# Loading a stage's constants one stage earlier, and issuing a load ahead of a store in one DMA queue

## What is computed

```python
x = x + conv3(conv2(conv1(group_norm(x))))      # 3x3, weights mixed per sample from 4 experts
# second layer, v = group_norm(x):
X  = dht2d(v)                                   # Hartley transform: real part minus imaginary part of the FFT
Xc = X[:, :, 96:160, 96:160]                    # 64 x 64 modes; Xrc the same of the flipped transform
x_even, x_odd = (Xc + Xrc) * 0.5, (Xc - Xrc) * 0.5
total = einsum('bixy,ioxy->boxy', x_even, kernel) + einsum('bixy,ioxy->boxy', x_odd, flipped_kernel)
out = dht2d(pad(total), is_inverse=True) + bias # back to 256 x 256
x = x + out
```

## Time and profile before

| | |
|---|---|
| median of 3 runs | 4815.48 us (4814.95 to 4819.85) |
| the profiled execution | 4815.04 us, span 4813.2 us |
| TensorE busy over the span | 4398.2 us (91%) |
| VectorE, ScalarE, GpSimd | 77%, 53%, 36% |
| DMA, inverse stage (4111.6 to 4813.2 us) | 396 GB/s |
| DMA, mixing stage (3783.0 to 4111.6 us) | 168 GB/s |

### The profile page before, as it was taken

The page is one execution under the profiler, slowest core; times in us unless marked ns, Lnnn a source line. Parts: engine busy times, 40 slices in busy tenths (PEclk is TensorE's granted clock), DMA queues, the critical chain, the costliest instruction groups (busy, mean ns, idle before and its releaser), DMA issues. The chain is left out here.

```text
span 4813.2 us, 126429 instructions
## 1 busy us (share of the span) xinstructions
PE 4398.2 (91%) x43186; PEld 2826.4 (59%) x43186; DVE 3683.3 (77%) x5717; ACT 2549.5 (53%) x4890; POOL 1726.5 (36%) x1963
## 2 busy tenths in 40 slices
PE   5999999999999999999999999995887677799998
PEld 2555555555555555555555545454777677688887
DVE  5877877878778787787877877777888799565555
ACT  2666666566566665666666656565787300233333
POOL 4455454554545545455454554544000000000000
PEclk9999999999999999999999999998999788899999
DMA  5867668676686766867767777679999798899999
GB/s 143 198 153 176 168 158 191 147 181 168 151 191 155 183 166 144 191 158 181 170 149 181 171 166 170 146 182 261 330 338 328 186 198 159 326 406 404 406 406 378
DMA packets 730995, 1042.38 MB, mean 217 GB/s; under 512 B 149184, under 2 KB 612832, under 8 KB 680928
## 3 DMA queue, kind: packets, MB, share of 16 engines
q1 hardware_dynamic: 658064, 1011.11, 75.8%
q10 hardware_dynamic: 72784, 29.63, 2.4%
HBM read 746.67 MB, written 293.88 MB: 216 GB/s over the span
## 5 line engine op out<-in xcount | busy, mean ns | idle before, releaser
L350 PE MATMUL bank<-ring_B,w_now 128*64 128x512 f16 (+1 forms) x14283 | 3091.0, 377 | 90.9 <-DVE ring_B L292 60.2
L350 PE MATMUL bank<-ring_A,w_now 128*64 128x512 f16 (+1 forms) x14283 | 3091.2, 377 | 0.0
L350 PEld LDWEIGHTS bank<-ring_B,w_now 128*64 128x64 f16 x14283 | 1547.5, 109 | 1517.7 <-issue 73.0
L350 PEld LDWEIGHTS bank<-ring_A,w_now 128*64 128x64 f16 x14283 | 1547.4, 109 | 0.0
L288 ACT COPY ring_B<-ring_A 64x516 f32<-64x516 f32 x1059 | 657.7, 621 | 944.3 <-DVE ring_A L574 906.0
L574 DVE SCALAR_TENSOR_TENSOR ring_A<-bank,ring_A 128x512 f16<-128x512 f32 (+1 forms) x1027 | 700.5, 682 | 463.8 <-ACT ring_A L418 444.1
L418 ACT ACTIVATE ring_A<-bank 128x512 f16<-128x512 f32 (+1 forms) x1027 | 603.0, 587 | 275.3 <-PE bank L350 273.0
L728 POOL TENSOR_TENSOR ring_A<-xn,ring_A 128x512 f16<-128x512 f32 x515 | 584.7, 1135 | 94.6 <-POOL xn L726 92.7
L1427 DVE SCALAR_TENSOR_TENSOR i_ot<-i_ob,i_bias_bc,i_xt 128x512 f32<-128x512 f32 x512 | 363.8, 747 | 294.8 <-DMA i_xt<-x 184.5
L1371 PE MATMUL i_ob<-i_back,i_u 128*128 128x256 f32 x2048 | 529.2, 381 | 10.8 <-DVE i_ot L1427 9.3
L290 ACT COPY ring_B<-ring_A 64x516 f32<-64x516 f32 x705 | 438.3, 622 | 8.1
(11 more groups left out here) (161 smaller groups left out, 5148.8 us busy)
## 6 DMA issues: line engine op xcount, KB each, us to landing
f_xt<-x SPq DMA_DIRECT2D x128, 1024.0 KB, 6.0
i_xt<-x SPq DMA_DIRECT2D x128, 1024.0 KB, 16.2
out<-i_ot SPq DMA_DIRECT2D x128, 1024.0 KB, 14.2
st_in_A<-in_x SPq DMA_DIRECT2D x65, 1024.0 KB, 7.4
st_in_B<-in_x SPq DMA_DIRECT2D x65, 1024.0 KB, 7.8
x_in_A<-in_x SPq DMA_DIRECT2D x324, 192.0 KB, 4.0
res_A<-in_x SPq DMA_DIRECT2D x324, 192.0 KB, 5.2
res_B<-in_x SPq DMA_DIRECT2D x324, 192.0 KB, 5.0
```

Source lines behind the costliest of these rows:

```text
L350: last = nc.tensor.matmul(dst[64 * half:64 * half + 64, 0:nb * IMG], w_now[n][:, w, 64 * dx:64 * dx + 64], r[side][:, kind, s0:s0 + nb, dx ...
```

## The change

Two edits, both in the diff below. First, `back` and `bias_bc` are allocated ahead of the forward stage and kept to the end, and their two loads are issued by ScalarE, as the first instructions of its stream in `build_mix`, with a semaphore of their own; ScalarE waits for them at the end of its stream there. The two loads and the semaphore `here` disappear from `build_inverse`, with the waits of TensorE and VectorE on it. Second, in each group of `build_inverse` SP issues the load of `x1` first and the store behind it; both stand behind the same wait for `o_ready`.

```diff
@@ build_mix
         @block.scalar
         def _(act):
+            act.dma_start(back[:], spec[:, OFF_BACK:OFF_BACK + 2 * IMG]).then_inc(consts_here, 16)
+            act.dma_start(bias_bc[:], bias.rearrange("c a b -> (a b) c").to_broadcast([P, C])).then_inc(consts_here, 16)
+
             for k in range(NCK):
                 act.wait_ge(emptied, k + 3)
                 for g in range(2):
                     y0 = 32 * g + k * T
                     act.dma_start(t_d[:, y0:y0 + T].rearrange("b t o x -> (t o) b x"), to[:, g]).then_inc(gone, 16)
+            act.wait_ge(consts_here, 32)
@@ build_inverse
-        back = sb("back", [P, 2 * IMG])
-        bias_bc = sb("bias_bc", [P, C])
...
             load_t(0)
-            sp.dma_start(back[:], spec[:, OFF_BACK:OFF_BACK + 2 * IMG]).then_inc(here, 16)
-            sp.dma_start(bias_bc[:], bias.rearrange("c a b -> (a b) c").to_broadcast([P, C])).then_inc(here, 16)
             for g in range(NB):
                 sp.dma_start(xt[g][:], xv[0, :, 4 * g:4 * g + 4, :]).then_inc(x_here[g], 16)
...
                     sp.wait_ge(o_ready, n0 + (4 * g + 4 + O_READY))
+                    if not last or g < 8 - NB:
+                        at = s if g < 8 - NB else sp.snap(s + 1)
+                        k = 4 * ((g + NB) % 8)
+                        sp.dma_start(xt[g % NB][:], xv[at, :, k:k + 4, :]).then_inc(x_here[g % NB], 16)
                     sp.dma_start(ov[s, :, 4 * g:4 * g + 4, :], ot[g % NB][:]).then_inc(gone[g % NB], 16)
-                    if last and g >= 8 - NB:
-                        continue
-                    at = s if g < 8 - NB else sp.snap(s + 1)
-                    k = 4 * ((g + NB) % 8)
-                    sp.dma_start(xt[g % NB][:], xv[at, :, k:k + 4, :]).then_inc(x_here[g % NB], 16)
...
         @block.tensor
         def _(pe):
-            pe.wait_ge(here, 32)
-
...
@@ build_inverse, vector
-            dve.wait_ge(here, 32)
             with dve.Fori(0, S) as s:
@@ build
+        back = ctx.enter_context(nc.sbuf_tensor("i_back", [P, 2 * IMG], f32))
+        bias_bc = ctx.enter_context(nc.sbuf_tensor("i_bias_bc", [P, C], f32))
```

More of the change, by code:

```diff
@@ L1169, in _, with build_mix @@
             sample(S - 1, 1, True)
-def build_mix(nc, f_d, fm_d, w, t_d, wt, wr, S):
+def build_mix(nc, f_d, fm_d, w, t_d, wt, wr, back, bias_bc, spec, bias, S):
     f32 = mybir.dt.float32
@@ L1194, in build_mix @@
         gone = sem("gone")
+        consts_here = sem("consts_here")
         block = ctx.enter_context(nc.Block())
@@ L1277, in _, with build_inverse @@
                     act.dma_start(t_d[:, y0:y0 + T].rearrange("b t o x -> (t o) b x"), to[:, g]).then_inc(gone, 16)
-def build_inverse(nc, t_d, x1d, bias, spec, out_d, S):
+            act.wait_ge(consts_here, 32)
+def build_inverse(nc, t_d, x1d, back, bias_bc, out_d, S):
     f32 = mybir.dt.float32
@@ L1307, in build_inverse @@
         ob = [ps(f"ob{i}", [P, 512]) for i in range(4)]
-        here, zeroed, u_ps, u_ready, o_ps, o_ready = (sem(n) for n in ("here", "zeroed", "u_ps", "u_ready", "o_ps", "o_ready"))
+        zeroed, u_ps, u_ready, o_ps, o_ready = (sem(n) for n in ("zeroed", "u_ps", "u_ready", "o_ps", "o_ready"))
         t_here = sem("t_here")
@@ L1441, in build @@
     with ExitStack() as ctx:
[L1443 to L1447, removed]
+        back = ctx.enter_context(nc.sbuf_tensor("i_back", [P, 2 * IMG], f32))
+        bias_bc = ctx.enter_context(nc.sbuf_tensor("i_bias_bc", [P, C], f32))
+        with ExitStack() as inner:
+            weights = lambda name: inner.enter_context(nc.sbuf_tensor(name, [P, C, ROWS, M], f32))
+            wt, wr = [weights(f"m_wt{i}") for i in range(2)], weights("m_wr")
+            build_forward(nc, x1, x1_stats, spec, modes, middle, mode_w, wt[0], wr, S)
+            build_mix(nc, modes, middle, mode_w, mixed_modes, wt, wr, back, bias_bc, spec, bias, S)
+        build_inverse(nc, mixed_modes, x1, back, bias_bc, out, S)
 _INS = ["x", "L0_conv_w_c1", "L0_conv_w_c2", "L0_conv_weight1", "L0_conv_weight2", "L0_conv_weight3",
```

## The result

| | before | changed | ratio |
|---|---|---|---|
| median of 12 runs each | 4818.9 us (4808.6 to 4826.6) | 4801.1 us (4797.1 to 4812.3) | 0.9968, 95% interval 0.9959 to 0.9977 |
| the same, measured once more (14 and 8 runs) | 4812.9 us | 4795.7 us | 0.997, 0.9953 to 0.9987 |
| profiled execution, span | 4813.2 us | 4803.7 us | |

The change is faster by 0.32%, some 15 us (the two medians themselves lie 17.8 us apart, 17.2 us in the second measurement), and the forecast of 4813.3 us (4806.7 to 4820.2) is missed.

The account below looks back on a forecast made before the run. The prediction took TensorE, then from about 4286 us the DMA engines, to bound the inverse. 4815.04 - 2.2 + 0 + 0 = 4812.8 us, with the median 0.44 us above: 4813.3 us, range 4806.7 to 4820.2.

Parts of the forecast that it names:

- The bound: Inverse stage: TensorE sets the pace at first, DMA engines from about 4286 us, 42.94 us a sample at 404 GB/s.
- Edit 1 at the inverse's entry: Inverse's start: TensorE's first product no longer waits for the bias, 2.2 us earlier, all kept to the end.
- Edit 1 at the mixing's entry: Mixing's start: the two constant loads hide behind the clearing of ft, cost 0, at most 6.9 us.
- The Trainium skill's rule on shared engines: Mixing's entry: moving loads to another queue gains no bandwidth; forecast not to bite, since nothing is in flight there.
- Edit 2, "0 us for the 124 pairs": Inverse's groups: exchanging load and store leaves the bytes and VectorE's wait the same, 0 us.
- The swap of the waits: Inverse: VectorE's waits on x1 all but gone, replaced by about 175 us of waits on output stores.
- The end of the kernel: Last landing, now a store: taken as 0, between 1.7 us gained and 3.0 us lost.
- rival A: Inverse: the store's landing costs up to 3.0 us more than the load's, giving 4816.3 us; chance 0.12.
- Rivals C and D: C: longer round of four buffers, 4845 us, chance 0.05; D: constants delay first ft loads, 4820.2 us, chance 0.04.
- Rival B: Inverse: waits for x1 go away, pace becomes TensorE's, 17.3 us sooner, 4796 us; chance 0.05.
- The sum: Whole kernel: 4815.04 - 2.2 + 0 + 0 = 4812.8 us profiled, 4813.3 us as median.

Follow-up runs that it names:

- s1: Kernel before with only 2176 unused bytes a partition added ahead of the weights: 0.9994 (0.9985 to 1.0004) of the kernel before.
- i8: Inverse stage alone, store ahead of load, loads of tt after the first left out: 682.7 us.
- i10: Inverse stage alone, loads on either side of tt's place in the queue, loads of tt after the first left out: 682.1 us.
- i6: Inverse stage alone, load ahead of store in each sample's first group, store ahead in the seven others, so tt has stores on either side: 682.4 us.
- b1_best: Whole kernel with edit 1, ordered so that tt has a store on either side: 4784.9 us, 0.9947 (0.9933 to 0.996) of the kernel before.
- s2: Changed kernel with 6016 unused bytes a partition behind the constants: 0.9988 (0.9978 to 0.9999) of the kernel before.
- i9: Inverse stage alone, loads on either side of tt, tt in one DMA over 128 partitions in place of two over 64: 681.6 us.
- i5: Inverse stage alone, store ahead of load in each sample's first group, load ahead in the seven others, so tt has loads on either side: 717.3 us.
- i1: Inverse stage of the kernel before alone, store ahead of load, tt behind the load: 699.3 us.
- i2: Inverse stage alone with edit 2, load ahead of store, tt behind the store: 692.8 us.

## Why the prediction was wrong

- **The bound** was read rightly, and too coarsely: DMA-paced from 4286 us, 42.9 us a sample. I took 404 GB/s as the engines' rate. It is a mean over 417 GB/s for x1 and output (2 MiB in a group of 5.03 us) and a dip for tt, and the dip is what made the DMA engines the bound.
- **Edit 1 at the inverse's entry**: the mechanism was right, and 6.82 us to the first product is the 6.8 forecast. The 2.2 us stand against one profile with 9.00 us; against the four profiles without edit 1 the gain is 1.1 us in the mean. That the two profiles differ by just 2.2 is luck.
- **Edit 1 at the mixing's entry**: right in cost (0; SyncE's wait 8.9 us as before). The Trainium skill's rule on shared engines, quoted there, had nothing to bite on. What I left out is that the edit moves the arrays; this shortens the loads of the modes by 0.6 us, and by the total of `s1` it may be worth some 3 us (0.06% of 4818; the interval of `s1` holds 0 too). Its size stays open.
- **Edit 2, "0 us for the 124 pairs"**: the step that failed. It said that a queue worked through in order can't be made faster by re-ordering, since the bytes stay the same. That holds for the pairs (5.03 us a group in both; `i8`, `i10`), but tt stands in the same queue, and what it costs hangs on its neighbours. I did write that the change leaves tt's turn as it was, and that was true and beside the point: its neighbours were exchanged. Measured in the stage alone: 6.5 us, in place of 0.
- **The swap of the waits** came as told: x1 no longer waited for, the output's landing in its place (142.6 us, 175 forecast). The end of the kernel didn't lose: from the last group's start to the end it is 10.6 us in both profiles (4813.2 - 4802.62 by the earlier trace rows; 4803.7 - 4793.13 by the row here). So rival A found nothing, nor did the up to 2 us that the Trainium skill puts on the receipt of a write; the section quoted gives them for DMAs that GpSimd issues, and these are SyncE's. Rivals C and D didn't occur.

```profile
4793.13 0.75 DVE L1424 SCALAR_TENSOR_TENSOR i_ot<-i_ob,i_bias_bc,i_xt 128x512 f32<-128x512 f32 x1 [1.69 <-DMA out<-i_ot]
```

- **Rival B** (0.05) was held unlikely since it needed 417 GB/s where 404 were seen. `i6` moves 418 GB/s. The changed kernel got a part of the way there, `b1_best` all of it, by another reason than the rival's: in the changed kernel the waits for x1 went to the store, which had no slack, and in `b1_best` both are gone because tt no longer slows the stream. The 0.05 covered anything that makes the stream faster by over 9.6 us, so the outcome wasn't left out, it was held too unlikely.
- **The sum**: 1.1 + 6.5 us are 0.16%, and 0.22% with 3 us for the addresses, which no run shows clear of 0. The two edits measured apart in the whole kernel give 0.10 + 0.15 = 0.25%. The second measurement's interval (0.13 to 0.47%) holds all three, the first's (0.23 to 0.41%) only the last. What makes up the rest, and what `s2` lost, is open.

## What to carry to other kernels

A DMA share of 1.0 says that the engines have packets in hand, not that they move bytes at their best rate: look at the GB/s over one period in fine slices, and price each kind of transfer by its own dip. Where a re-ordering leaves the bytes alone, list the neighbours of every transfer in the queue, the small ones too. And load into all 128 partitions by one DMA, as in `i9`; where two halves can't be avoided, try them between stores, as in `b1_best`.

## What the hardware showed that was not expected

- 0.5 MiB moved as two DMAs over 64 partitions each cost 36 us in 16 samples when loads stood on both sides, 18 us with a load ahead and a store behind, 11 us the other way round, and nothing that shows behind TensorE's pace between stores (`i5`, `i1`, `i2` and `i6` against `i9`'s 681.6 us, to about 1 us).
- A packet of x1 that shared the engines with those halves took 416 ns in place of 311 (`i5`); beside the same bytes in one DMA over 128 partitions it took 309 (`i9`).
- 2176 bytes of shift in the partitions' address brought the shortest landing of a 512 KB store from 3.9 to 3.4 us and the median of a 128 KB load from 5.1 to 4.4 us; a shift by 8192 bytes did not (4.0 and 5.1 us; `before`, `s1` and `s2`).
